# Second mixer of a two-layer block: where each LayerNorm's transposes stand beside the batch's two products

## The chip, the cores and the metric

The kernel runs on 1 core of one Trainium2 chip. The metric is the device time of one execution in microseconds; the kernel before took 2007.04 us, the median of 3 runs (2003.31 to 2009.59). TensorE is called PE below, VectorE DVE, ScalarE ACT, GpSimd POOL and SyncE SP.

## The reference, cut to what matters

Two layers, each `x = x + ga * mixer(LN(x)(1+ca)+sa)` and then `x = x + gb * ffn(LN(x)(1+cb)+sb)`, on x of 4 batches x 512 tokens x 512 features. Layer 0 has linear attention and a mixture of 8 experts. Layer 1, where the change lies, has

```
mixer(h) = h + rmsnorm(y) * norm_w
y        = h @ M          # M (512 x 512): both projections and the elementwise coefficients, made in the kernel
ffn(h)   = sparsify_2to4(silu(h @ w_gate) * (h @ w_up)) @ w_down      # inner size 2048, 2 largest of each 4 kept
```

So one batch of the second mixer is `x += ga*h + rmsnorm(h @ M)*norm_w*ga`: a dense product for y, a product of h with a diagonal matrix (the gate) for `ga*h`, and the root mean square of y.

## The kernel before, in words

Five queues run one hand-written order (`walk`): prologue, 8 groups x 4 batches of attention (stage A), routing, 39 expert slots, `back`, then `step_c` for 4 batches (stage C, the second mixer), then `step_d` for 4 groups x 4 batches (stage D, the second feed-forward), and an end. Every engine has its own list in that order, and they meet on counted semaphores only.

Each float32 product is made of three matmuls on a high and a low part (`mm3`, L744 to L746). A product of 512 tokens therefore needs its input normalised, transposed and split. For one LayerNorm, named (k, b) by kind and batch (k = 2 is the mixer's, k = 3 the feed-forward's), the steps are: DVE takes mean and variance (`c_stats`) and runs a chain of 11 or 12 tiny operations for the scales (`c_scales`); ACT writes the four normalised tiles into `xw` or `xn` (`ln_scaled`, L1373); PE makes 16 transposes of 128x128 into four PSUM slots (`ln_transposes`, L775); ACT takes each slot to `tmp` (L1171) and rounds it to the high part of `hT` (L1175) (`ln_out`); POOL subtracts for the low part (`lo_part`, L2053). `need_h` makes PE wait for the last of these.

The PSUM slots are a ring of two banks (`TAIL`). Everything that passes through the ring has a number from `plan_ring`, the same for all engines; slot n may be written once slot n-2 has been read. The LayerNorm's slots are read by ACT, the diagonal product's four slots ("res") by DVE, which adds them to x (L1970).

In `back`, PE makes M (64 matmuls of 512 columns from `mst`, L1030) and then the transposes of LayerNorms (2,0) and (2,1).

In `step_c(b)`, PE does y (4 tiles of 12 matmuls of 128x512 into six PSUM banks), then the diagonal product `gated_h` (4 tiles of 12 matmuls of 128x128, into ring slots), then the 16 transposes of the LayerNorm in `C_LNS[b]`. ACT first normalises the next LayerNorm, then squares and sums the four y tiles (`squares`, L1383), then empties the transposes. DVE does the statistics, then the scale chain for both the LayerNorm and y (it waits for the squares, L1928), then the four adds that empty the ring (L1970), then scales y into `yn` (L1975), and adds it to x (L1982). POOL marks the res slots and makes the low parts.

In the first `step_d(0, 0)`, r = 0 to 3 counts the four gate/up pairs of a group (24 matmuls of 128x512 each, weights in W1a and W1b). The transposes of (3,1), (3,2) and (3,3) stand behind r = 0, 1 and 3 (`D_LNS`). After r = 3 DVE runs the 2:4 selection on the four products (L2006 to L2033). PE's pair r may begin when DVE has emptied pair r-2 (`d_h`), also across batches.

Of the kernel before, what the change touches and what calls it, by code (L numbers as in the profile page):

```python
# [55 lines left out]
MOD_FINISH = [(0, 1, 2), (3,), (4,), (9,)]  # L56
MOD_PLACE = [(0, 0), (0, 1), (0, 2), (1, 0), (1, 2), (2, 0), (2, 1), (2, 2), (3, 0), (3, 2)]

C_LNS = [(2, 2), (2, 3), (3, 0), None]
D_LNS = {0: (3, 1), 1: (3, 2), 3: (3, 3)}  # L60
STATS = [(2, 0), (2, 1), (2, 2), (2, 3), ("y", 0), (3, 0), ("y", 1), (3, 1), ("y", 2), (3, 2), ("y", 3), (3, 3)]

NSA, NSE, NSD = 4, 4, 6
# [68 lines left out]
def tail_of(stage, g, b):  # L132
# [5 lines left out]
    if isinstance(g, int) and g == 0:  # L138
# [5 lines left out]
ROUTES = [("rt", 0), ("pf", 0)]  # L144
FRONT = [("rt", 1), ("tail", *LAST_A), ("ln", 1, 2, 0), ("ln", 1, 2, 1), ("pf", 1), ("rt", 2),
         ("ln", 1, 3, 0), ("ln", 1, 3, 1), ("pf", 2), ("rt", 3), ("pf", 3)]
BACK = [("ln", 2, b, h) for b in range(2) for h in range(2)]


def plan_ring():  # L150

    at, n = {("ln", 0, 0, 0): 0, ("ln", 0, 0, 1): 2}, 4
    size = {"tail": NT, "ln": NC // 2, "mod": 1, "rt": 1, "pf": 1, "res": NT}
    for stage, groups in (("A", GA), ("B", 0), ("C", 1), ("D", GD)):
        for part in FRONT + BACK if stage == "B" else []:
            at[part] = n
            n += size[part[0]]
        for g in range(groups):
            for b in range(NB):
                tail, ln = tail_of(stage, g, b), layernorms(stage, g, b)  # L160
                parts = [("tail", *tail)] if tail else []
                if ln:

                    halves = [("ln", *ln, 0), ("ln", *ln, 1)]
                    parts = halves[:1] + parts + halves[1:]
                if stage == "C":
                    parts = [("res", b)] + ([("ln", *C_LNS[b], h) for h in range(2)] if C_LNS[b] else [])
                if (stage, g, b) == ("D", 0, 0):
                    parts = [("ln", *ln, h) for ln in D_LNS.values() for h in range(2)]
                if stage == "A" and g == 0:  # L170
                    mods = [[("mod", *use) for use in mod_uses(0, b, k)] for k in range(3)]
                    parts = mods[0] + mods[1] + (halves if ln else []) + mods[2] + ([("tail", *tail)] if tail else [])
                if (stage, g, b) == LAST_A:
                    parts = ROUTES + parts
                for part in parts:
                    at[part] = n
                    n += size[part[0]]
    at[("tail", "D", GD - 1, 3)] = n
    return at
# [51 lines left out]
def build(nc, x_in, wa, wbe, wdn, winout, coef, cT, wmod0, wmod1, gwT, bo, norm_w, out, rows_d_):  # L231
# [4 lines left out]
    with ExitStack() as ctx:  # L236
# [504 lines left out]
        def _(pe):  # L741
# [280 lines left out]
            def back():  # L1022
                pe.wait_ge(m_scaled, 8)
                for half, banks in ((0, (0, 1)), (1, (4, 5))):
                    if half == 0:
                        pe.wait_ge(s_p, SLOTS)
                    for ic in range(8):
                        for j in range(2):
                            m = 2 * half + j
                            last = pe.matmul(bank[banks[j]][:, :], mst[:, ic, m * P:(m + 1) * P], mst[:, ic, 512:1024],  # L1030
                                             start=ic == 0, stop=ic == 7)
                    last.then_inc(m_full, 1)
                for b in range(2):
                    for half in range(2):
                        ln_transposes((2, b), half)

            def gated_h(b):

# [9 lines left out]
            def step_c(b):  # L1048
                need_h(2, b)
                if b == 0:  # L1050
                    pe.wait_ge(m_lo, 4)
                    pe.wait_ge(y_evac, SLOTS)
                for t in range(NT):
                    n = NT * b + t
                    if n >= 6:
                        pe.wait_ge(y_read, n - 5)
                    for c in range(NC):
                        last = mm3(bank[YB[n % 6]][:, :], hcol(c, b, t), lambda h, c=c: M[:, h, c, :],
                                   c == 0, c == NC - 1)
                    last.then_inc(y_full, 1)  # L1060
                gated_h(b)
                for half in range(2):
                    ln_transposes(C_LNS[b], half)


            def tail_d(g, b, n0):
# [11 lines left out]
            def step_d(g, b):  # L1078
                s = g * NB + b
                first = isinstance(g, int) and g == 0  # L1080
                if first:
                    need_h(3, b)
                for r in range(4):
                    if first and b == 0 and r < 2:
                        pe.wait_ge(y_read, (NT * NB - 4, NT * NB)[r])
                    if b == 0:
                        pe.wait_ge(split_done, split_d_at(g, r) + 1)
                    if not (first and b == 0 and r < 2):
                        pe.wait_ge(d_h, s * 4 + (r - 1))
                    for u, o, full in ((0, bank[r % 2], dg_full), (1, bank[4 + r % 2], du_full)):  # L1090
                        for c in range(NC):
                            last = mm3(o[:, :], lambda h, c=c: gud[r // 2][:, r % 2, h, u, c, :], hrow(c, b),
                                       c == 0, c == NC - 1)
                        last.then_inc(full, 1)
                    if first and b == 0 and r in D_LNS:
                        ln_transposes(D_LNS[r], 0)
                        ln_transposes(D_LNS[r], 1)
                tails("D", g, b)

            def epi():  # L1100
# [6 lines left out]
        def _(act):  # L1107
# [236 lines left out]
            def back():  # L1344
# [14 lines left out]
                ln_out((2, 0), 0)  # L1359
                ln_out((2, 0), 1)  # L1360
                ln_scaled(2, 1)
                ln_out((2, 1), 0)
                ln_out((2, 1), 1)

            def ln_scaled(k, b):

# [19 lines left out]
            def step_c(b):  # L1386
                if b > 0:
                    ln_scaled(*((2, 3), (3, 0), (3, 1))[b - 1])
                squares(b)
                if b == 0:  # L1390
                    ln_scaled(2, 2)
                if b == 3:
                    act.wait_ge(ring_full, RING[("res", 3)] + NT)
                    split_d(0, 2)
                    split_d(0, 3)
                if C_LNS[b]:
                    ln_out(C_LNS[b], 0)
                    ln_out(C_LNS[b], 1)

            def step_d(g, b):  # L1400
                s = g * NB + b
# [13 lines left out]
                for r in range(4):  # L1415
# [6 lines left out]
                    if b == 3 and not (isinstance(g, int) and g == GD - 1):  # L1422
                        act.wait_ge(du_full, s * 4 + (r + 1))
                        split_d(g + 1, r)
                    if first and b == 0:
                        if r in D_LNS:
                            if r > 0:
                                ln_scaled(*D_LNS[r])
                            ln_out(D_LNS[r], 0)
                            ln_out(D_LNS[r], 1)  # L1430
                    elif r > 0:
                        absolute(r - 1)
                for r in range(4) if first and b == 0 else (3,):
                    absolute(r)
                if tail_of("D", g, b):
                    act.wait_ge(ring_full, ring_before("D", g, b) + NT)
                if first and b == 0:
# [12 lines left out]
        def _(dve):  # L1450
# [504 lines left out]
            def step_c(b):  # L1955
                if b == 0:
                    c_stats(2, 2)
                    c_stats(2, 3)
                    c_scales((2, 2), (2, 3), ("y", 0))
                else:  # L1960
                    c_stats(3, b - 1)
                    c_scales((3, b - 1), ("y", b))
                n0 = RING[("res", b)]
                for t in range(NT):
                    n = n0 + t
                    if t == 0:
                        dve.wait_ge(ring_read, n)
                    dve.wait_ge(ring_full, n + 1)
                    xt = x[:, NT * b + t, :]
                    dve.tensor_tensor(xt, TAIL[n % 2][:, :], xt, ALU.add).then_inc(ring_read, 1)  # L1970
                dve.wait_ge(crow_full, 16 * (b + 1))
                col = column(("y", b))
                for t in range(NT):
# [10 lines left out]
            def step_d(g, b):  # L1984
                s = g * NB + b
                for r in range(4):
                    dve.wait_ge(du_full, s * 4 + (r + 1))
                    dve.wait_ge(d_silu, s * 4 + (r + 1))
                    dve.tensor_tensor(hh[:, r, :], hh[:, r, :], bank[4 + r % 2][:, :], ALU.mult).then_inc(d_h, 1)  # L1989
                    if isinstance(g, int) and g == 0 and b == 0 and r == 1:  # L1990
                        c_stats(3, 3)
                        c_scales((3, 3))
                done = [0]
# [57 lines left out]
        def _(pool):  # L2051
# [244 lines left out]
            def back():  # L2296
                split_d(0, 0)
                split_d(0, 1)
                for b in range(2):
                    ln_out((2, b), 0)  # L2300
                    ln_out((2, b), 1)

            def step_c(b):
                n0 = RING[("res", b)]
                for t in range(NT):
                    pool.wait_ge(ring_done, n0 + t)
# [2 lines left out]
                if b == 3:  # L2309
                    split_d(0, 2)  # L2310
                    split_d(0, 3)
                ln_out(C_LNS[b], 0)
                ln_out(C_LNS[b], 1)

            def step_d(g, b):
                s = g * NB + b
# [1 line left out]
                    for j in range(4):  # L2318
                        split_d(g + 1, j)
                if isinstance(g, int) and g == 0 and b == 0:  # L2320
                    for ln in D_LNS.values():
                        ln_out(ln, 0)
                        ln_out(ln, 1)
                tails("D", g, b)
                for r in range(4):
                    if isinstance(g, int) and g == GD - 1 and b == NB - 1:
# [63 lines left out]
```

## Time and profile before

| | before |
|---|---|
| median of 3 runs | 2007.04 us |
| the profiled execution: its own time / its span | 2002.69 us / 2000.9 us |
| mean granted PE clock | 0.953 of 2.4 GHz |
| busy: PE / DVE / ACT / POOL | 92% / 60% / 36% / 34% |

"Busy" is the share of the span in which an engine executed something; a row of the timeline has the start in us from the span's start, the duration, engine, source line, operation and tiles, the count where like ones are merged, and in square brackets the idle time before it with the instruction that ended it. The granted clock is 1.00 at 2.4 GHz and 0.50 at 1.2 GHz; a value between is a stretch that had both. Stage C with its run-up lies between 1310 and 1412 us, the first step of stage D between 1412 and 1467.

### The profile page before, as it was taken

The page shows a single profiled execution, that of the slowest core. Times are in us where ns is not written, and L with a number is a line of the kernel's source. Part 1 is how long each engine was busy: PE and PEld are TensorE (multiplying, and loading weights), DVE is VectorE, ACT ScalarE, POOL GpSimd, SP SyncE. Part 2 cuts the span into 40 slices and gives each one's busy share as a digit, 9 for nine tenths or more (in the row PEclk, how much of TensorE's full clock was granted, in tenths as well). Part 3 has the DMA queues.
Part 4 walks back from the last instruction along what each step waited for, and adds up shares of the span by engine and source line. Part 5 has one row for each costly group of instructions (what it writes and reads, how often), then busy time and mean ns, then how long its engine had stood idle before and what let it go on. Part 6 is the DMA issues. An engine that isn't in the chain of part 4 may idle for free. (4 is left out here: it accounts for less than half of the span.)

```text
span 2000.9 us, 25863 instructions
## 1 busy us (share of the span) xinstructions
PE 1842.2 (92%) x8492; PEld 1450.2 (72%) x8492; DVE 1191.6 (60%) x2112; ACT 716.7 (36%) x1369; POOL 686.3 (34%) x697
## 2 busy tenths in 40 slices
PE   8989999999999999998457898989889999999996
PEld 5657888888888888876356676657768778787784
DVE  4557666666666666677853343647465747566664
ACT  2434454445444444433112232355523122213220
POOL 1435121212112222111353555533344445435442
PEclk9999999999999999998758998988999999999998
DMA  6221454435353525421375999610001011101011
GB/s 237 79 71 60 138 159 130 152 95 164 90 189 105 189 82 186 126 85 37 106 258 162 334 267 261 159 52 11 27 27 42 17 32 48 31 5 53 6 53 42
DMA packets 101122, 218.46 MB, mean 109 GB/s; under 512 B 8640, under 2 KB 33232, under 8 KB 99504
## 3 DMA queue, kind: packets, MB, share of 16 engines
q1 hardware_dynamic: 78848, 168.70, 26.0%
q0 software_dynamic: 11584, 28.97, 6.1%
q10 hardware_dynamic: 10608, 19.74, 3.1%
q8 instruction: 45, 0.74, 0.1%
q14 instruction: 37, 0.30, 0.0%
HBM read 126.02 MB, written 91.37 MB: 109 GB/s over the span
## 5 line engine op out<-in xcount | busy, mean ns | idle before, releaser
L744 PE MATMUL bank<-hT,W1b 128*128 128x512 f32 x512 | 208.9, 408 | 14.8 <-DVE hh L1989 14.8
L1743 DVE RECIPROCAL rr<-rr 128x256 f32<-128x256 f32 x128 | 218.8, 1730 | 4.7 <-ACT num L1212 4.7
L744 PE MATMUL bank<-W1a,hT 128*128 128x512 f32 x512 | 209.7, 410 | 3.4 <-DVE hT L1657 3.4
L745 PE MATMUL bank<-hT,W1b 128*128 128x512 f32 x512 | 204.0, 399 | 0.0
L746 PE MATMUL bank<-hT,W1b 128*128 128x512 f32 x512 | 203.6, 398 | 0.0
L746 PE MATMUL bank<-W1a,hT 128*128 128x512 f32 x512 | 202.0, 395 | 0.0
L745 PE MATMUL bank<-W1a,hT 128*128 128x512 f32 x512 | 201.2, 393 | 0.0
L2115 POOL TENSOR_TENSOR x<-x,tmp 128x512 f32<-128x512 f32 x64 | 101.3, 1583 | 272.2 <-DVE tmp L1735 272.2
L1989 DVE TENSOR_TENSOR hh<-hh,bank 128x512 f32<-128x512 f32 x64 | 43.4, 686 | 195.4 <-PE bank L746 166.0
L1762 DVE SCALAR_TENSOR_TENSOR kt<-bank,kt 128x256 fp32r<-128x256 f32 x128 | 50.8, 397 | 173.9 <-ACT vt L1228 173.7
L2053 POOL TENSOR_TENSOR W<-stage,W 128x1024 fp32r<-128x1024 f32 x32 | 76.9, 2404 | 189.5 <-ACT W L1131 187.2
L1227 ACT ACTIVATE kt<-bank 128x256 fp32r<-128x256 f32 x128 | 49.3, 385 | 235.7 <-PE bank L746 235.0
L1441 ACT ACTIVATE ad<-hh 128x512 fp32r<-128x512 f32 x64 | 40.3, 633 | 255.3 <-DVE hh L2033 255.3
L744 PE MATMUL bank<-W1b,ot 128*128 128x512 f32 x256 | 104.8, 410 | 23.0 <-DVE tmp L1732 14.8
L744 PEld LDWEIGHTS bank<-hT,W1b 128*128 128x128 f32 x512 | 97.6, 191 | 38.9 <-DVE hh L1989 17.5
L744 PEld LDWEIGHTS bank<-W1a,hT 128*128 128x128 f32 x512 | 97.2, 190 | 37.0 <-issue 15.5
L746 PEld LDWEIGHTS bank<-hT,W1b 128*128 128x128 f32 x512 | 97.3, 190 | 23.9
L746 PEld LDWEIGHTS bank<-W1a,hT 128*128 128x128 f32 x512 | 97.1, 190 | 22.1
L745 PEld LDWEIGHTS bank<-hT,W1b 128*128 128x128 f32 x512 | 97.5, 190 | 19.8
L744 PE MATMUL bank<-W,ad 128*128 128x512 f32 x256 | 102.8, 402 | 9.0 <-DVE ad L2040 8.9
L745 PEld LDWEIGHTS bank<-W1a,hT 128*128 128x128 f32 x512 | 97.4, 190 | 17.7
L1796 DVE SCALAR_TENSOR_TENSOR qt<-bank,qt 128x512 fp32r<-128x512 f32 x64 | 44.0, 690 | 102.6 <-ACT qt L1256 102.6
(274 smaller groups left out, 4644.0 us busy)
## 6 DMA issues: line engine op xcount, KB each, us to landing
hs_d<-bor SPq DMA_DIRECT2D x24, 1548.0 KB, 11.3
ws_d<-W SPq DMA_DIRECT2D x48, 512.0 KB, 6.3
WB<-ws_d SPq DMA_DIRECT2D x8, 3072.0 KB, 17.9
stage<-wa SPq DMA_DIRECT2D x32, 512.0 KB, 5.3
stage<-wbe SPq DMA_DIRECT2D x24, 512.0 KB, 4.2
stage<-wdn SPq DMA_DIRECT2D x24, 512.0 KB, 3.9
mw<-wmod SPq DMA_DIRECT2D x10, 1024.0 KB, 5.0
hg<-hs_d ACTq DMA_DIRECT2D x39, 258.0 KB, 5.7
```

Of the source, the lines that this page charges most:

```text
L744: pe.matmul(o, lhs(HI), rhs(HI), start=start, stop=False, **kw)
L745: pe.matmul(o, lhs(HI), rhs(LO), start=False, stop=False, **kw)
L746: return pe.matmul(o, lhs(LO), rhs(HI), start=False, stop=stop, **kw)
L1227: act.activation(kt[:, t % 2, HI, :], bank[t % 2][:, 0:256], ACT.Relu)
L1441: act.activation(ad[:, r, HI, :], hh[:, r, :], ACT.Copy).then_inc(d_hi, 1)
L1743: dve.reciprocal(rr[:, pair, h], rr[:, pair, h]).then_inc(r_rec, 1)
L1762: dve.scalar_tensor_tensor(out=kt[:, t % 2, LO, :], in0=bank[t % 2][:, 0:256], scalar=0.0, in1=kt[:, t % 2, HI, :].bitcast(F32), op0=ALU.m ...
L1796: dve.scalar_tensor_tensor(out=qt[:, LO, pair, :], in0=bank[pair][:, :], scalar=0.0, in1=qt[:, HI, pair, :].bitcast(F32), op0=ALU.max, op1 ...
L1989: dve.tensor_tensor(hh[:, r, :], hh[:, r, :], bank[4 + r % 2][:, :], ALU.mult).then_inc(d_h, 1)
L2053: return pool.tensor_tensor(dst, src, hi.bitcast(F32), ALU.subtract)
L2115: pool.tensor_tensor(xt, xt, tmp[:, (key + t) % 2, :], ALU.add).then_inc(ring_done, 1)
```

## The change

Each LayerNorm of the mixer moves one place earlier in the order, each batch's transposes stand between y and the diagonal product, DVE's adds stand ahead of its scale chain, and the three LayerNorms of `step_d(0, 0)` stand behind r = 0 (two) and r = 1 (one). No instruction is added or taken out.

```diff
-C_LNS = [(2, 2), (2, 3), (3, 0), None]
-D_LNS = {0: (3, 1), 1: (3, 2), 3: (3, 3)}
+C_LNS = [(2, 1), (2, 2), (2, 3), (3, 0)]
+D_LNS = [[(3, 1), (3, 2)], [(3, 3)], [], []]
-BACK = [("ln", 2, b, h) for b in range(2) for h in range(2)]
+BACK = [("ln", 2, 0, h) for h in range(2)]
 # plan_ring
-                    parts = [("res", b)] + ([("ln", *C_LNS[b], h) for h in range(2)] if C_LNS[b] else [])
+                    parts = [("ln", *C_LNS[b], h) for h in range(2)] + [("res", b)]
...
 # PE, back
-                for b in range(2):
-                    for half in range(2):
-                        ln_transposes((2, b), half)
+                for half in range(2):
+                    ln_transposes((2, 0), half)
 # PE, step_c
-                gated_h(b)
                 for half in range(2):
                     ln_transposes(C_LNS[b], half)
+                gated_h(b)
 # PE, step_d
-                    if first and b == 0 and r in D_LNS:
-                        ln_transposes(D_LNS[r], 0)
-                        ln_transposes(D_LNS[r], 1)
+                    if first and b == 0:
+                        for ln in D_LNS[r]:
+                            ln_transposes(ln, 0)
+                            ln_transposes(ln, 1)
 # ACT, back
                 ln_scaled(2, 1)
-                ln_out((2, 1), 0)
-                ln_out((2, 1), 1)
 # ACT, step_c
                 squares(b)
+                ln_out(C_LNS[b], 0)
+                ln_out(C_LNS[b], 1)
                 if b == 0:
                     ln_scaled(2, 2)
                 if b == 3:
                     act.wait_ge(ring_full, RING[("res", 3)] + NT)
                     split_d(0, 2)
                     split_d(0, 3)
-                if C_LNS[b]:
-                    ln_out(C_LNS[b], 0)
-                    ln_out(C_LNS[b], 1)
 # ACT, step_d, after silu of pair r
-                    if first and b == 0:
-                        if r in D_LNS:
-                            if r > 0:
-                                ln_scaled(*D_LNS[r])
-                            ln_out(D_LNS[r], 0)
-                            ln_out(D_LNS[r], 1)
-                    elif r > 0:
+                    for ln in D_LNS[r] if first and b == 0 else []:
+                        if ln != (3, 1):
+                            ln_scaled(*ln)
+                        ln_out(ln, 0)
+                        ln_out(ln, 1)
+                    if first and b == 0 and r == 2:
+                        absolute(0)
+                    if r > (1 if first and b == 0 else 0):
                         absolute(r - 1)
-                for r in range(4) if first and b == 0 else (3,):
-                    absolute(r)
+                absolute(3)
 # DVE, step_c: the chain goes behind the four adds
-                    c_scales((2, 2), (2, 3), ("y", 0))
...
-                    c_scales((3, b - 1), ("y", b))
...
                     dve.tensor_tensor(xt, TAIL[n % 2][:, :], xt, ALU.add).then_inc(ring_read, 1)
+                c_scales(*([(2, 2), (2, 3)] if b == 0 else [(3, b - 1)]), ("y", b))
 # DVE, step_d
-                    if isinstance(g, int) and g == 0 and b == 0 and r == 1:
+                    if isinstance(g, int) and g == 0 and b == 0 and r == 0:
                         c_stats(3, 3)
                         c_scales((3, 3))
```

POOL's `back`, `step_c` and `step_d` follow the same order: `ln_out(C_LNS[b])` moves to the head of `step_c`, ahead of the res marks and of `split_d(0, 2)` and `split_d(0, 3)`.

## Rows read from the trace of the kernel before

**Rows 1.** The page, part 1: engine, busy us (share of the span), instructions.

```profile
PE 1842.2 (92%) x8492; PEld 1450.2 (72%) x8492; DVE 1191.6 (60%) x2112; ACT 716.7 (36%) x1369; POOL 686.3 (34%) x697
```

**Rows 2.** Busy time by stretch: stretch, length, busy us (instructions) by engine, clock, DMA.

```profile
1335.40:1347.70 12.30, 10.70 (x66) 9.55 (x64) 7.69 (x21) 6.33 (x10) 2.01 (x5) 0.72 0.00 0
1358.70:1370.50 11.80, 10.34 (x67) 9.16 (x65) 7.79 (x21) 3.46 (x7) 2.13 (x6) 0.75 0.00 1
1382.00:1392.70 10.70, 9.25 (x65) 8.10 (x64) 7.38 (x21) 3.20 (x6) 1.78 (x5) 0.84 0.00 0
1403.70:1412.00 8.30, 7.05 (x51) 6.87 (x49) 3.91 (x15) 0.69 (x2) 0.55 (x3) 0.82 0.00 0
1417.00:1443.70 26.70, 23.36 (x115) 18.43 (x114) 13.94 (x26) 17.58 (x27) 11.89 (x9) 1.00 0.12 38
```

**Rows 3.** Timeline of PE, run-up and stage C.

```profile
1314.16 0.66 PE L775 MATMUL bank<-ident,xw 128*128 128x128 f32 x4 [0.67 <-ACT tmp L1171]
1320.56 3.15 PE L775 MATMUL bank<-ident,xnb 128*128 128x128 f32 x12 [5.74 <-ACT xnb L1373]
1324.33 0.48 PE L744 MATMUL bank<-M_,hT 128*128 128x512 f32 x1
...
1335.41 0.22 PE L744 MATMUL bank<-dg,hT 128*128 128x128 f32 x1
1337.93 0.27 PE L746 MATMUL bank<-dg,hT 128*128 128x128 f32 x1
1339.58 0.33 PE L744 MATMUL bank<-dg,hT 128*128 128x128 f32 x1 [1.38 <-DVE x L1970]
...
1340.75 0.41 PE L745 MATMUL bank<-dg,hT 128*128 128x128 f32 x1
1343.52 0.41 PE L746 MATMUL bank<-dg,hT 128*128 128x128 f32 x1
...
1358.78 0.22 PE L744 MATMUL bank<-dg,hT 128*128 128x128 f32 x1
...
1382.01 0.22 PE L744 MATMUL bank<-dg,hT 128*128 128x128 f32 x1
...
1403.79 0.22 PE L744 MATMUL bank<-dg,hT 128*128 128x128 f32 x1
```

**Rows 4.** Timeline of DVE, batch 0: head of the chain, then the adds.

```profile
1336.40 0.17 DVE L1928 TENSOR_SCALAR cst<-csum 128x4 f32<-128x4 f32 x1 [17.35 <-ACT sqj L1383]
...
1338.84 1.29 DVE L1970 TENSOR_TENSOR x<-bank,x 128x512 f32<-128x512 f32 x2
```

**Rows 5.** Timeline of ACT: slots 1 and 3 of (2,0), and the last square of batch 0.

```profile
1311.99 0.78 ACT L1171 ACTIVATE tmp<-bank,modc 128x512 f32<-128x512 f32 x1
...
1314.91 0.78 ACT L1171 ACTIVATE tmp<-bank,modc 128x512 f32<-128x512 f32 x1
...
1335.61 0.60 ACT L1383 ACTIVATE sqj<-bank 128x512 bf16<-128x512 f32 x1 [2.06 <-PE bank L746]
```

**Rows 6.** Timeline of POOL: the last two low parts of (2,0).

```profile
1316.43 2.59 POOL L2053 TENSOR_TENSOR hT<-tmp,hT 128x512 fp32r<-128x512 f32 x2 [0.32 <-ACT hT L1175]
```

**Rows 7.** Timeline of PE, first step of stage D.

```profile
1411.97 0.73 PE L744 MATMUL bank<-hT,W1a 128*128 128x512 f32 x1
...
1415.88 0.39 PE L744 MATMUL bank<-hT,W1a 128*128 128x512 f32 x1
...
1419.33 1.03 PE L775 MATMUL bank<-ident,xnb 128*128 128x128 f32 x8
...
1422.59 0.48 PE L744 MATMUL bank<-hT,W1a 128*128 128x512 f32 x1
```

**Rows 8.** Timeline of ACT, one LayerNorm normalised, stage D.

```profile
1426.36 2.92 ACT L1373 ACTIVATE xw<-x,cst 128x512 f32<-128x512 f32 x4
```

**Rows 9.** Timeline of DVE: the first selection begins.

```profile
1452.29 0.85 DVE L2006 TENSOR_TENSOR fl<-xnb 128x512 bf16<-128x512 f32 x1 [7.47 <-ACT xnb L1413]
```

**Rows 10.** Timeline of PE: the third pair of batch 1 begins.

```profile
1466.76 0.79 PE L744 MATMUL bank<-hT,W1b 128*128 128x512 f32 x1 [7.49 <-DVE hh L1989]
```

More of the change, by code:

```diff
@@ L166, in plan_ring @@
                 if stage == "C":
-                    parts = [("res", b)] + ([("ln", *C_LNS[b], h) for h in range(2)] if C_LNS[b] else [])
+                    parts = [("ln", *C_LNS[b], h) for h in range(2)] + [("res", b)]
                 if (stage, g, b) == ("D", 0, 0):
-                    parts = [("ln", *ln, h) for ln in D_LNS.values() for h in range(2)]
+                    parts = [("ln", *ln, h) for lns in D_LNS for ln in lns for h in range(2)]
                 if stage == "A" and g == 0:
@@ L2298, in back @@
                 split_d(0, 1)
-                for b in range(2):
-                    ln_out((2, b), 0)
-                    ln_out((2, b), 1)
+                ln_out((2, 0), 0)
+                ln_out((2, 0), 1)
             def step_c(b):
+                ln_out(C_LNS[b], 0)
+                ln_out(C_LNS[b], 1)
                 n0 = RING[("res", b)]
@@ L2311, in step_c @@
                     split_d(0, 3)
-                ln_out(C_LNS[b], 0)
-                ln_out(C_LNS[b], 1)
             def step_d(g, b):
@@ L2320, in step_d @@
                 if isinstance(g, int) and g == 0 and b == 0:
-                    for ln in D_LNS.values():
-                        ln_out(ln, 0)
-                        ln_out(ln, 1)
+                    for lns in D_LNS:
+                        for ln in lns:
+                            ln_out(ln, 0)
+                            ln_out(ln, 1)
                 tails("D", g, b)
```

## The prediction

> **What bounds the kernel now.** I read the page first: PE is busy for 92% of the span, the next engine for 60% [rows 1], so what counts is where PE waits and at which clock it runs. Next the stretches around the change: in each batch of stage C the part behind y runs at a granted clock of 0.72 to 0.84, while the first step of stage D, three sets of transposes included, runs at 1.00 [rows 2]. Then the timeline of PE, to see why. I call E(b) the moment when y of batch b is issued and what follows it begins: E(0) to E(3) are 1335.41, 1358.78, 1382.01 and 1403.79 [rows 3]. In batch 0 the first two diagonal tiles go out as 24 matmuls, the last of them 2.52 us behind the first: 0.11 us each. The third waits 1.38 us for DVE, which is in its scale chain from 1336.40 to 1338.8 and only then empties the ring [rows 3, 4]. The other three batches have the same wait. The reader is to see what comes behind it: from 1340.75 the same matmuls take (1343.52 - 1340.75) / 13 = 0.213 us. The clock has gone from 2.4 to 1.2 GHz, 5.3 us after E(0), behind two tiles that keep PE half fed and one short wait. Rows 2 say the same of the other batches.
>
> **The change part by part.**
>
> *Start of the stage.* Before, PE stood still from 1314.6 until ACT had normalised (2,1), made its transposes at 1320.56 and began y(0) at 1324.33 [rows 3]. Now y(0) needs only (2,0), whose last low part POOL ends at 1316.43 + 2.59 = 1319.02 [rows 6]. y takes 1335.41 - 1324.33 = 11.08 us [rows 3]. PE has then idled for 4.5 us and starts slow. The nearest price is the first pair of stage D: nine matmuls from 1411.97 to 1415.88 took 3.91 us [rows 7] where nine at the full clock take 9 x 11.08 / 48 = 2.08, a loss of 1.8. E(0) comes at 1319.1 + 11.1 + 1.8 = 1332.0: 3.4 us earlier (5.2 without the slow start).
>
> *Behind y: the transposes.* The last square begins 0.20 us behind E and lasts 0.60 [rows 5] and 0.15 to 0.35 for reading out its sum and changing over, so ACT takes the first slot at E + 0.95. It takes the third slot 2.92 us after the first and needs 0.78 for it [rows 5]: E + 4.65. The diagonal product's first slot is the one that follows that, so it cannot start before E + 4.7, where before it started at E. Up to there PE has only 16 transposes, some 1.65 us of work. That is 3.0 us of idle in three pieces of 0.9 to 1.2.
>
> *The diagonal product.* DVE has nothing in front of the adds now and empties a tile in 0.65 [rows 4] against 1.34 for making one: the 1.38 us wait goes, in four batches. At the full clock the 48 matmuls take 5.35 us and end at E + 10.1; need_h is met (POOL ends at about E + 8 to 9, its four low parts 7.0 us behind ACT's first slot as in rows 5 and 6). At 1.2 GHz they take 48 x 0.213 = 10.2 and end at E + 14.9.
>
> *Which clock.* This decides. In all four batches of before the clock fell during the diagonal product, with 1.38 us or less of idle beside it [rows 2, 3]. The new order puts 3.0 us of idle right ahead of the same half-fed matmuls, so I expect a fall no later than before. The rows against it are those of stage D, where 16 transposes took 3.26 us [rows 7], 1.6 of it idle, and the clock stayed at 1.00 [rows 2]; but there dense pairs stand on both sides. I take the fall at E + 5.3, the soonest of the four: 0.6 us at full clock (5 matmuls), then 43 x 0.213 = 9.1. The product ends at E + 14.4. The bounds are 10.1 and 14.9. Then y of the next batch begins slow, again 1.8 (0 to 2.8).
>
> The Trainium skill (TensorE: Matmul & The Clock Gate, "HAM oscillation") lays the fall to one long idle gap. By that rule the gaps of 1.2 us here would do nothing, and the first rival below would be the outcome; this case's trace disagrees, since its clock fell behind 1.38 us. The same page ("A second HAM failure mode") says that many micro-idles between groups of matmuls make the clock swing, and with that the trace agrees.
>
> *Sum to E(3).* A batch takes 14.4 + 11.1 + 1.8 = 27.3 us; three are 81.9, where before E(0) to E(3) was 68.38 [rows 3]: +13.5. DVE keeps up: its chain (2.4), yn (2.7), adds to x and statistics end 12 us behind the product, in y's shade, where nothing waits.
>
> *Into stage D.* From E(3) to the end of pair 0 it was 1419.33 - 1403.79 = 15.54 us [rows 3, 7], without a LayerNorm between. Now it has one: 14.4 + 5.5 + 1.8 = 21.7, +6.2. At the end of pair 0 we stand at -3.4 + 13.5 + 6.2 = +16.3.
>
> *First step of stage D*, from the end of pair 0, T. Before: 1466.76 - 1419.33 = 47.4 until PE resumes behind the selection [rows 7, 10]. Now two LayerNorms stand behind pair 0, but ACT normalises (3,2) only when it has emptied (3,1): 0.7 + 5.8 + 2.9 [rows 5, 8] = T + 9.45, while PE is through with (3,1) at T + 3.3 [rows 7]. PE idles 6.2 us and the transposes run slow (3.8, as 1320.56 to 1324.33 [rows 3]): T + 13.4. Pair 1 takes 5.6 + 0.9 (half a slow start), a wait of 0.8 for (3,3), its transposes 3.3, pairs 2 and 3 11.2: T + 35.2 against T + 28.8 before. Here the work was not on the path: before, the selection began only at 1452.29, T + 33.0, as ACT had (3,3) to do first [rows 9]. Now it begins 1.0 behind pair 3, at T + 36.2, and from there to the resumption it is 1466.76 - 1452.29 = 14.5 [rows 9, 10]: T + 50.7, +3.3 (2 to 5). The remaining steps of stage D only shift.
>
> *DMA.* None is added. SP's loads of crow and of the next weights keep their places in its queue and wait for the same events; with a DMA share of 0.00 beside the mixer [rows 2] I count them at nothing. POOL makes two weight splits (5 us) behind the res marks of batch 3 as before, and pair 2 is the first to need them.
>
> *Total.* 16.3 + 3.3 = +19.6 us. Against the profiled execution's own 2002.69 that is 2022.3. That execution lies 4.35 under the median of the three runs, 2007.04, and the sum upon the median is 2026.6. I say 2024. It splits as -5.0 + 6.1 for each batch whose clock falls, since one at the full clock takes 10.1 + 11.1 = 21.2 instead of 27.3.
>
> **The rivals.**
>
> 1. *The clock holds (other side).* PE's transposes and the unbroken diagonal product keep 2.4 GHz. Then 3 x 21.2 = 63.6 against 68.4, with -3.4 at the start, nothing between E(3) and T (10.1 + 5.5), +3.3 in stage D: -5.0, 1998 to 2002. It decides if fewer than one batch in four falls. For it: the wait of 1.38 is gone and stage D's transposes never cost the clock. Against: 3.0 us of idle take its place.
> 2. *The clock falls in half of the batches*, or late in each: -5.0 + 2 x 6.1 = +7.2, 2012.
> 3. *The clock holds, and stage D costs all of its PE delay*, the selection giving no cover: 35.2 - 28.8 = 6.4 in place of 3.3: -1.9, about 2003, no change.
>
> **How the numbers follow.** Forecast 0.60, rival 1 0.17, rival 2 0.15, rival 3 0.08. All four batches slow for the whole product with a slow start of 2.8 gives 2 x 4 = 8 us more, 2034; the forecast's own range is 2012 to 2034. Reaching to the rivals the range is 2003 to 2034. Within 0.3% (6 us, about what a measurement tells) lie rival 3 and half of rival 1: 0.15. Rival 1's faster half and what I have missed: 0.11. Slower: 0.74.
>
> **What would show it.** Granted clock between E and the next y: below 0.75 in each batch if I am right, 1.00 if rival 1 is. First diagonal matmul 4.7 us behind E, with no wait for DVE in it. E(0) near 1332, E to E 27 us (21 for rival 1). PE idle for 6 us ahead of the transposes of (3,2). The selection starting 1 us behind pair 3. I am wrong if the diagonal matmuls are 0.111 us apart throughout, or if the transposes are emptied faster than ACT's pace here.

## The result, and the profile after

The changed kernel takes 2027.25 us (median of 4 runs, 2022.06 to 2029.61), the kernel before 2005.17 on the same chip; the ratio is 1.0104, with a 95% interval of 1.0077 to 1.013. By the ratio that is 21 us slower (22 between the two medians). The forecast was 2024. The profiled execution took 2027.44 us, with a span of 2025.7, and the mean granted clock went from 0.953 to 0.944.

The stretches that answer to [rows 2], each from E to 16.7 us behind it, and then the first step of stage D in two parts (columns as there):

```profile
1334.70:1351.40 16.70, 14.44 (x71) 13.23 (x70) 4.05 (x12) 5.99 (x10) 5.82 (x8) 0.66 0.00 1
1362.20:1378.90 16.70, 14.44 (x71) 13.25 (x70) 3.93 (x12) 5.99 (x10) 5.81 (x8) 0.66 0.00 0
1389.70:1406.40 16.70, 14.44 (x70) 13.34 (x69) 3.79 (x11) 5.99 (x10) 5.82 (x8) 0.65 0.00 0
1417.20:1433.90 16.70, 14.44 (x70) 13.35 (x69) 3.72 (x8) 7.74 (x12) 6.44 (x9) 0.64 0.01 6
...
1439.20:1453.00 13.80, 6.04 (x34) 4.50 (x32) 13.63 (x22) 11.02 (x16) 7.26 (x5) 0.75 0.13 38
...
1461.30:1466.00 4.70, 3.94 (x19) 3.11 (x19) 0.00 (x0) 3.70 (x6) 2.35 (x2) 0.68 0.00 0
```

The clock falls in all four batches. The timeline of PE shows how in batch 0; it answers to [rows 3]:

```profile
1321.22 0.80 PE L744 MATMUL bank<-M_,hT 128*128 128x512 f32 x1 [4.25 <-POOL hT L2049]
...
1334.74 1.03 PE L775 MATMUL bank<-ident,xnb 128*128 128x128 f32 x8
1336.35 0.66 PE L775 MATMUL bank<-ident,xnb 128*128 128x128 f32 x4 [0.57 <-ACT tmp L1171]
1337.68 0.66 PE L775 MATMUL bank<-ident,xnb 128*128 128x128 f32 x4 [0.67 <-ACT tmp L1171]
1339.35 0.30 PE L744 MATMUL bank<-dg,hT 128*128 128x128 f32 x1 [1.01 <-ACT tmp L1171]
...
1340.18 0.41 PE L745 MATMUL bank<-dg,hT 128*128 128x128 f32 x1
...
1348.71 0.41 PE L746 MATMUL bank<-dg,hT 128*128 128x128 f32 x1
1348.92 0.73 PE L744 MATMUL bank<-M_,hT 128*128 128x512 f32 x1
1349.46 0.63 PE L745 MATMUL bank<-M_,hT 128*128 128x512 f32 x1
1349.88 0.63 PE L746 MATMUL bank<-M_,hT 128*128 128x512 f32 x1
```

E(0) is 1334.74. The diagonal product starts 4.6 us later, and no DVE wait is left in it. From E + 5.4 its matmuls are 0.213 us apart, and it ends at E + 14.2; in the other batches the clock falls at E + 5.4, 5.1 and 4.9, and the product ends at E + 14.3 to 14.7. The next y begins at 0.43 us a matmul instead of 0.23. E to E is 27.48, 27.50 and 27.50 us.

"Half-fed" is short for this: a 128x128 matmul goes out every 0.111 us at the upper clock and every 0.213 us at the lower one, a 128x512 matmul every 0.23 and 0.43 us. So the diagonal product needs about half of the time for a quarter of the columns.

In stage D (answers to [rows 7, 10], timeline of PE) there are the idle of 6.3 us ahead of (3,2), and one of 2.6 ahead of (3,3):

```profile
1439.23 1.03 PE L775 MATMUL bank<-ident,xnb 128*128 128x128 f32 x8
...
1449.06 3.15 PE L775 MATMUL bank<-ident,xw 128*128 128x128 f32 x12 [6.33 <-ACT xw L1371]
...
1461.33 1.09 PE L775 MATMUL bank<-ident,xnb 128*128 128x128 f32 x8 [2.64 <-ACT xnb L1371]
...
1492.06 0.80 PE L744 MATMUL bank<-hT,W1b 128*128 128x512 f32 x1 [4.07 <-DVE hh L1985]
```

Times within the stage are best counted from the first transposes of (2,0), S, because S itself lies anywhere from 1309.9 to 1315.7 in the profiled executions of these kernels. I call T the end of pair 0 and R the resumption behind the first selection. Before, S is 1310.82, the start of those transposes in that trace.

| | S to E(0) | E(0) to E(3) | E(3) to T | T to R | S to R |
|---|---|---|---|---|---|
| before | 24.6 | 68.4 | 15.5 | 47.4 | 155.9 |
| after | 21.8 | 82.5 | 22.0 | 52.8 | 179.1 |

S to R costs 23.2 us more in these two executions.

### The profile page after: what moved, and what is told of

The parts are those of the page before. It is cut to its first block and busy times, and to the rows that moved or that the text cites. A ratio compares the mean times of both kernels' runs of the same rounds, so it can differ in the third digit from the quotient of the medians.

```text
span 2025.7 us, 25863 instructions
## 1 busy us (share of the span) xinstructions
PE 1857.0 (92%) x8492; PEld 1465.2 (72%) x8492; DVE 1186.8 (59%) x2112; ACT 716.0 (35%) x1369; POOL 682.4 (34%) x697
## 5 line engine op out<-in xcount | busy, mean ns | idle before, releaser
L744 PE MATMUL bank<-W1b,ot 128*128 128x512 f32 x256 | 105.2, 411 | 21.9 <-DVE tmp L1729 14.1
L744 PEld LDWEIGHTS bank<-hT,W1b 128*128 128x128 f32 x512 | 97.8, 191 | 35.4 <-DVE hh L1985 14.1
L745 PEld LDWEIGHTS bank<-hT,W1b 128*128 128x128 f32 x512 | 97.6, 191 | 19.8
```

Of the source, the lines that this page charges most:

```text
L744: pe.matmul(o, lhs(HI), rhs(HI), start=start, stop=False, **kw)
L745: pe.matmul(o, lhs(HI), rhs(LO), start=False, stop=False, **kw)
```

## The experiments

Theory 1 is that of the prediction: the clock, pulled down by idle ahead of the half-fed diagonal product. Theory 2 is that this product is slow for its place, and the clock a consequence. All ratios are to the kernel before, run on the same chip.

**All gaps filled** (`fill_all`). The changed kernel, with matmuls whose result nobody reads. `fill(4)` also stands between slots 3 and 4 and behind the last; `fill` first waits until `yn` has read the bank, which the cut leaves out:

```diff
+def fill(count):        # into a y bank that yn has read (the wait is left out here)
+    for _ in range(count):
+        pe.matmul(bank[YB[(NT * b + 4) % 6]][:, :], hT[:, HI, 0, b * S:b * S + P], M[:, HI, 0, :], start=True, stop=True)
 ln_transposes(C_LNS[b], 0)
+fill(4)
```

> The changed kernel with 4 idle-filling matmuls of 128x512 (0.23 us each, results never read) in each of the three gaps of the transposes behind y: 12 per batch, 48 in all, more work for PE and nothing removed. Theory 1 (the loss is the clock, which falls because 3 us of idle stand ahead of the half-fed diagonal product): granted clock 1.00 between E and the next y, diagonal matmuls 0.111 us apart, E to E 21.1 instead of 27.5 us, and about 24 us less than the changed kernel: about 2003, ratio to the kernel before 0.998 to 1.001. Theory 2 (the diagonal product is slow for its place in the order or for the slots it waits for, and the clock only follows): E to E stays at 27.5 us or grows by the fillers, ratio 1.010 or more.

Measured: 1998.40 us, ratio 0.9966 (0.9952 to 0.9979). Busy time by stretch, E(0) and 10 us:

```profile
1333.60:1343.60 10.00, 10.00 (x78) 9.14 (x76) 2.08 (x3) 6.00 (x10) 5.68 (x7) 1.00 0.01 2
```

Twelve more matmuls a batch, and a batch takes 21.1, 21.3 and 21.1 us instead of 27.5, with the diagonal product where the change put it, waiting for the same slots. Theory 2 is out. The gain over the changed kernel is 1.4%, some 28 us, 4 more than expected; 2.4 of these lie between T and R. Dummy matmuls do two things at once: they take idle away and add dense work. This run doesn't tell which of the two held the clock.

**Only the last gap filled** (`fill_last`).

```diff
 ln_transposes(C_LNS[b], 1)
+fill(4)
 gated_h(b)
```

At the other two places `fill(0)` stands: no matmul, but its wait for `yn` is there. The first gap is 0.66 to 0.93 us in batches 1 to 3, against 0.57 in the changed kernel.

> The changed kernel with 4 such matmuls in the last of the three gaps alone, directly ahead of the diagonal product; 2 us of idle stay. Theory 1, if what counts is the idle just ahead of the diagonal product: the clock holds in all four batches, as with all gaps filled (ratio about 1.000). Theory 1, if the whole stretch counts: it holds in some batches and falls in others (ratio 1.003 to 1.008). Theory 2: ratio 1.010 or more.

Measured: 1999.32 us, ratio 0.9980 (0.9965 to 0.9995); the clock is 1.00 in all four stretches, of which batch 1's is

```profile
1354.60:1365.00 10.40, 8.74 (x70) 7.76 (x69) 2.52 (x8) 6.44 (x12) 5.69 (x7) 1.00 0.00 0
```

A third of the dummy work, directly ahead of the diagonal product, is enough: 1.3 to 1.7 us of idle stay in each stretch and do nothing.

**The kernel before, its one wait filled** (`before_fill`). Five such matmuls between the second and the third diagonal tile, again behind a wait for a free bank.

```diff
 for t in range(NT):          # gated_h
+    if t == 2:
+        fill(5)
```

> The kernel before with 5 idle-filling matmuls of 128x512 (0.23 us each, results never read) where PE waits 1.3 us for DVE between the second and the third diagonal tile. If that one idle is what makes the clock fall in the kernel before, it now holds: E to E 21 us instead of 23.4, 23.2 and 21.8, and with E(3) to the end of pair 0 at 12.5 instead of 15.5 about 8 us less, ratio 0.996. If the half-fed diagonal product alone does it: ratio 1.000 and the same granted clock of 0.72 to 0.84 behind E.

Measured: 1996.04 us, ratio 0.9962 (0.9950 to 0.9974), and 21.5, 21.4 and 21.4 us a batch. So in the kernel before the clock did not fall for the diagonal product alone, but only with that wait in it. `adds_first` below shows the same without any added work. Answers to the first row of [rows 2]:

```profile
1335.80:1346.20 10.40, 9.06 (x70) 7.77 (x69) 7.25 (x21) 6.11 (x10) 1.76 (x5) 1.00 0.00 0
```

**The stage D part undone** (`d_undone`). ACT's absolute values and DVE's chain for (3,3), one pair later, stand as before too.

```diff
-D_LNS = [[(3, 1), (3, 2)], [(3, 3)], [], []]
+D_LNS = [[(3, 1)], [(3, 2)], [], [(3, 3)]]
```

> The changed kernel with the part in the first step of stage D undone: (3,1), (3,2), (3,3) behind pairs 0, 1, 3 as before. If the stage D part costs what the changed kernel's trace shows (52.8 us from the end of pair 0 to the resumption, where before it was 47.4), 5.4 us come back: about 2021, ratio 1.0075. If the idle there was hidden by the selection, as rival 3 has it in reverse, nothing moves: ratio 1.010.

Measured: 2020.23 us, ratio 1.0092 (1.0064 to 1.0121); T to R is 46.7 us, 6.1 less than in the changed kernel, and S to R falls by the same 6.1. The interval overlaps that of the changed kernel, so the ratios alone would allow no gain; the stretch shows it, in one profiled execution of each. With all gaps filled as well (`fill_d_undone`):

> The changed kernel with all three gaps filled (as in the first of these runs) and the stage D part undone. If the two terms are independent, the ratio is that of the filled kernel, 0.9966, less the 3 to 5 us of the stage D part: 0.994 to 0.995. If the selection covers the stage D part once the clock holds: 0.9966.

Measured: 1998.20 us, ratio 0.9971 (0.9956 to 0.9986), the same as `fill_all`. T to R is 50.4 in `fill_all`, 49.5 in `fill_last` and 49.4 here, so at most 1.0 us is left of the stage D part: with the clock held, T comes before DVE has yn of batch 3, and pair 1 waits 1.38 us for it and then runs slow for its first nine matmuls (7.3 us for the pair). The two terms are not independent.

**The DVE part undone** (`chain_first`). The scale chain ahead of the adds again, in the changed kernel.

```diff
+c_scales(*([(2, 2), (2, 3)] if b == 0 else [(3, b - 1)]), ("y", b))
 for t in range(NT):          # the four adds
...
-c_scales(*([(2, 2), (2, 3)] if b == 0 else [(3, b - 1)]), ("y", b))
```

> The changed kernel with the DVE part undone: the scale chain stands ahead of the four adds again. Theory 1 (in the new PE order the adds cannot begin before E + 7, and the chain needs only E + 0.9 to E + 3.3, so the part that the change is named for does nothing there): E to E stays at 27.5 us and the ratio to the kernel before at 1.010; yn is ready 2.4 us earlier, which may give back up to 2 us in the first step of stage D. Theory 2 (the adds ahead of the chain carry a gain of their own, 4 x 1.3 us, hidden by the clock's loss): 5 us slower than the changed kernel, 1.0125.

Measured: 2020.88 us, ratio 1.0071 (1.0047 to 1.0095). A batch takes 27.5, 27.7 and 27.5 us, as before this edit; T to R falls from 52.8 to 48.5. The two ratios' intervals overlap, but the stretch shows it: in the new PE order the DVE part of the change brings nothing and costs 4 us. The timelines of DVE and POOL say how, first in the changed kernel:

```profile
1433.28 4.91 POOL L2049 TENSOR_TENSOR W1b<-stage,W1b 128x1024 fp32r<-128x1024 f32 x2
...
1433.36 2.32 DVE L1929 TENSOR_TENSOR cst<-cst 128x8 f32<-128x8 f32 x1
1435.92 2.30 DVE L1931 SCALAR_TENSOR_TENSOR cst<-cst 128x8 f32<-128x8 f32 x1
...
1439.54 2.72 DVE L1971 SCALAR_TENSOR_TENSOR yn<-bank,cst,crow 128x512 f32<-128x512 f32 x4
1442.17 6.11 DVE L1978 TENSOR_TENSOR x<-x,yn 128x512 f32<-128x512 f32 x4
...
1448.80 2.46 DVE L1908 BATCH_NORM_STATS2 st<-x 128x6 f32<-128x512 f32 x4
...
1458.15 0.16 DVE L1933 SCALAR_TENSOR_TENSOR cst<-cmv,cst 128x4 f32<-128x4 f32 x1
```

and with the DVE part undone:

```profile
1434.28 2.72 DVE L1971 SCALAR_TENSOR_TENSOR yn<-bank,cst,crow 128x512 f32<-128x512 f32 x4
...
1442.28 2.46 DVE L1908 BATCH_NORM_STATS2 st<-x 128x6 f32<-128x512 f32 x4
...
1449.42 0.16 DVE L1933 SCALAR_TENSOR_TENSOR cst<-cmv,cst 128x4 f32<-128x4 f32 x1
```

In the changed kernel batch 3's chain stands behind the adds and runs while POOL splits weights (1433.28 to 1438.2), and two of its 0.17 us operations take 2.3. yn begins at T + 0.3 instead of T - 6.2, the scales of (3,3) are there at T + 18.9 instead of T + 9.0, PE waits 2.64 us instead of 0.78, and loses the clock once more (0.68 above; 1.00 in `chain_first`). The Trainium skill (SBUF — State Buffer, "SBUF: two separate sides") says that VectorE and GpSimd share a port pair, and that whichever of a VectorE instruction with two inputs in SBUF and a GpSimd instruction that reads SBUF starts first keeps it for its whole length. The rows agree: the stretched operations take both inputs from `cst` and end with POOL's two subtractions of 2.45 us, while yn in `chain_first`, which reads a PSUM bank, takes 0.68 us a tile beside the same weight split (1434.80 to 1440.0 there), as it does in the changed kernel without it.

`chain_first` shows one thing more. In its batches 2 and 3 the clock is down at the first diagonal matmul:

```profile
1395.69 0.44 PE L744 MATMUL bank<-dg,hT 128*128 128x128 f32 x1 [1.01 <-ACT tmp L1171]
1395.94 0.42 PE L745 MATMUL bank<-dg,hT 128*128 128x128 f32 x1
```

So behind y the 16 transposes with their three gaps are enough for the fall, without any half-fed matmul.

**DVE's order alone, on the kernel before** (`adds_first`).

```diff
 if b == 0:
     c_stats(2, 2)
     c_stats(2, 3)
+    c_scales((2, 2), (2, 3))
-else:
-    c_stats(3, b - 1)
-c_scales(...)
 # the four adds
+if b > 0:
+    c_stats(3, b - 1)
+c_scales(*([(3, b - 1)] if b > 0 else []), ("y", b))
```

> The kernel before with one part of the change alone: DVE empties the diagonal product's slots ahead of the scale chain (and of the next statistics; in batch 0 the LayerNorm's part of the chain runs early by itself). The order on PE stays as it was: y, diagonal product, transposes. Theory 1: without the wait of 1.3 us no idle stands beside the diagonal product, so the clock holds too: E to E falls from 23.4, 23.2 and 21.8 to 19.8 us and E(3) to the end of pair 0 from 15.5 to 11.0: 13 us less than before, about 1992, ratio 0.9935. If the diagonal product alone pulls the clock down, only the waits go: 5 us less, ratio 0.9975. If DVE becomes late for its new order (adds, statistics, chain, yn and x need 17 to 20 us of a batch): between the two or no gain.

Measured: 1997.72 us, ratio 0.9982 (0.9968 to 0.9996). The clock holds through the four batches, with nothing added to PE's work: the wait was what pulled it down in the kernel before. But yn is late: two batches wait 0.9 us, and pair 1 of stage D 4.24. It was the third case. So in the next one (`stats_first`) the statistics stay ahead of the adds, and only the chain stands behind them:

```diff
     c_scales((2, 2), (2, 3))       # batch 0
+else:
+    c_stats(3, b - 1)
 # the four adds
-if b > 0:
-    c_stats(3, b - 1)
 c_scales(*([(3, b - 1)] if b > 0 else []), ("y", b))
```

> The kernel before with DVE's order of the change (statistics, adds, then one scale chain) and batch 0's LayerNorm scales taken early; PE's order as before: y, diagonal product, transposes. The run with the adds ahead of the statistics kept the clock at 1.00 but made PE wait for yn: 0.9 us in two batches and 4.2 us in front of pair 1. With the statistics taken ahead of the adds these go: 6 us less than that run, about 1991 to 1992, ratio 0.994 to 0.995, E to E 19.9 us. If the waits for yn stay: 0.998.

Measured: 1991.01 us, ratio 0.9933 (0.9914 to 0.9953), 19.9 us a batch, E(3) to T 10.8. The waits for yn in the batches are gone, one of 1.37 us ahead of pair 1 is left.

**Transposes inside y** (`inside_y`), and all of them behind tile 1 (`mid_y`). In the changed kernel, with stage D as before and batch 0's scales early:

```diff
 # PE, inside the loop over the tiles t of y; ACT's ln_out likewise behind its square t
+if t in {0: (0,), 2: (1,)}:        # mid_y: {1: (0, 1)}
+    ln_transposes(C_LNS[b], 0 if t == 0 else 1)
...
-for half in range(2):
-    ln_transposes(C_LNS[b], half)
 gated_h(b)
```

> The change rearranged: each LayerNorm's 16 transposes stand inside y, 8 behind tile 0 and 8 behind tile 2, the diagonal product directly behind y; ACT empties them between its squares; DVE as in the change with batch 0's LayerNorm scales taken early; stage D as before. No matmul waits for a ring slot, and what idle is left stands between dense tiles. Theory 1: granted clock 1.00 through the four batches, 5.4 + 11.1 + 1.6 = 18.1 us a batch, the end of pair 0 at 20 us earlier than in the kernel before, some 1 to 2 us given back to a wait for yn: about 1986, ratio 0.990 to 0.992. If DVE is the next bound (adds, chain, yn, x, statistics: 17 to 20 us a batch): 19.5 to 20 us a batch, ratio 0.994.

> The same, but with all 16 transposes together behind tile 1 of y. The same two gaps of about 0.9 us for ACT's emptying are there as in the changed kernel, between dense tiles instead of ahead of the diagonal product. Theory 1 (it is the place of the idle, ahead of half-fed matmuls, that costs the clock): granted clock 1.00, 19.9 us a batch, ratio 0.993 to 0.995. If these gaps cost the clock wherever they stand: a granted clock under 0.9 in the batches, 22 us or more a batch, ratio above 0.998.

Measured: `inside_y` 1988.28 us, ratio 0.9916 (0.9892 to 0.9939), the lowest of all, though its interval overlaps that of `stats_first`; 18.1 us a batch with PE busy for the whole of it. `mid_y` 1999.15 us, ratio 0.9968 (0.9951 to 0.9986); 19.8, 21.1 and 22.7 us. First `inside_y`, then two batches of `mid_y` (the rows behind a long gap, then the stretches):

```profile
1357.20:1375.30 18.10, 18.10 (x113) 16.02 (x112) 12.73 (x33) 9.91 (x19) 5.06 (x8) 1.00 0.07 16
```

```profile
1368.62 0.66 PE L775 MATMUL bank<-ident,xnb 128*128 128x128 f32 x4 [1.83 <-ACT tmp L1172]
1389.67 0.66 PE L775 MATMUL bank<-ident,xw 128*128 128x128 f32 x4 [1.82 <-ACT tmp L1172]
```

```profile
1354.80:1375.90 21.10, 18.59 (x114) 16.09 (x113) 12.74 (x33) 10.80 (x20) 5.91 (x8) 1.00 0.04 14
1375.90:1398.50 22.60, 20.10 (x113) 17.14 (x113) 12.74 (x33) 10.88 (x20) 5.86 (x8) 0.92 0.03 12
```

In `mid_y` the gaps of batch 1 (0.57 and 0.68 us) leave the clock alone. In batches 2 and 3 ACT is late, the gaps are 1.83 and 0.68, and the clock falls in the second of the two and not in the first. So theory 1 in its strict form, that the place alone counts, is too strong: the amount seems to count too, and equal batches can differ. Executions differ as well: the seven lie between 1992.48 and 2002.59 us, and the profiled one took 1993.24. The wait ahead of pair 1 is another such pair: 1.38 us behind the same gaps, and the clock falls in `fill_d_undone` but holds in `stats_first`, `inside_y` and `mid_y` (1.37 to 1.38 us; 5.7 to 5.8 us for the pair, against 7.3). What decides between them no run shows.

From S to R, against 155.9 before, these profiles have: `fill_all` 151.1, `fill_last` 150.2, `before_fill` 147.8, `d_undone` 173.0, `fill_d_undone` 150.6, `chain_first` 174.6, `adds_first` 150.5, `stats_first` 142.8, `inside_y` 136.3, `mid_y` 147.3. The timed ratios, turned into us on 2005, lie within 5 us of these differences.

## Why the prediction was right

*Start of the stage.* Forecast 3.4 us earlier, measured 24.6 - 21.8 = 2.8: y(0) began after 4.25 us of idle (4.5), and the slow start cost 2.4 us instead of 1.8 (y took 13.52).

*Transposes and slots.* Right: the diagonal product at E + 4.6 (forecast 4.7). Its 3.0 us of idle are counted from issue to issue; as the profile counts, by which the wait before was 1.38, the three gaps are 2.25 us.

*The clock.* Right, and this carried the result: the fall at E + 4.9 to 5.4 (forecast 5.3, taken from the soonest row of before), in four of four batches, 0.213 us a matmul, the end at E + 14.2 to 14.7 (14.4), a slow start of y of 1.9 to 2.2 (1.8), a batch of 27.5 us (27.3). Three runs show it from both sides: filling the idle takes the loss away in the changed kernel and takes the old loss away in the kernel before; `adds_first` and `stats_first` take the wait itself away and the clock holds. For the changed kernel no run takes the gaps away and leaves the order, so that idle and not missing dense work is the cause there is argued from these. The prediction gave the half-fed product a share in the fall; `chain_first` shows that it isn't needed. And [rows 2] show two sets of stage D's transposes at 1.00, not three as the prediction has it; the third lies behind their window.

By the rule of one long idle gap of the Trainium skill (TensorE: Matmul & The Clock Gate, "HAM oscillation") the clock should have held, since no gap behind y exceeded 1.01 us; the measurement decides against it. By the same page of the Trainium skill ("A second HAM failure mode") frequent short idles between groups of matmuls make the clock swing; with three gaps a batch it did. In the kernel before a single wait a batch was enough, so the agreement that the prediction saw there was loose.

*Into stage D.* 22.0 us against the forecast 21.7.

*First step of stage D.* The idle ahead of (3,2) was 6.3 (6.2), and the selection began right behind pair 3, but at T + 38.5 and not T + 36.2, and T to R was 52.8 and not 50.7. The step that failed is "DVE keeps up": its chain, yn, adds to x and statistics were said to end where nothing waits. That holds for batches 0 to 2, not for batch 3, whose chain fell on POOL's weight split; (3,3) came late. The same sentence hid that the DVE part of the change costs 4.3 us: I counted it as freeing a wait of 1.38 us, but in the new order the first add comes at E + 6.8 to 7.4, and with the chain ahead of it (`chain_first`) the chain was done by E + 5.3 to 6.5. That the term came out only 2.1 too small is luck: with DVE in time T to R is 48.5, so the rest of the term was forecast 2.2 too large (the selection began 0.9 us sooner than forecast, and from there to R it was 13.2 us and not 14.5).

*The sum.* +19.6 forecast; 23.2 between the two profiled executions (-2.8 + 14.1 + 6.5 + 5.4), 21 by the ratio on 2005. All four terms came out above the forecast's -3.4 + 13.5 + 6.2 + 3.3. That 2024 lies as near as it does owes something to the step from 2022.3 towards the higher median. Rival 1 (the clock holds, -5.0) is what `fill_all` made real: -6.8 by its ratio. Rival 2 did not occur. Rival 3's price for stage D, 6.4, turned out near the 6.1 that `d_undone` gave back, but on top of the clock's loss.

The change was aimed at a real loss, the wait of 1.24 to 1.38 us in each batch and the clock that it costs. The PE part put three gaps in its place and turned the gain into a loss. DVE's order alone, with the statistics left ahead and batch 0's LayerNorm scales taken early (`stats_first`), takes 0.67% off.

## What to carry to other kernels

In this kernel one wait of 1.24 to 1.38 us amid half-fed matmuls cost PE its full speed, for up to 1.9 us a batch over the same product with the wait filled, and 2.25 us in three pieces ahead of them cost 6.4. Put short work that waits for another engine's emptying between dense matmuls, and nothing that makes PE wait ahead of narrow ones. When an order is changed, ask of each engine what it now waits for first: here the adds that were moved ahead had nothing to be ahead of.

## What the runs showed of the hardware that was not expected

Dummy matmuls paid for themselves: 4 per batch (`fill_last`), 0.9 us of PE's time that was idle anyway, gained 6.4 us a batch. Taking the wait away in the kernel before (`stats_first`, 142.8 us from S to R) was still better than filling it (`before_fill`, 147.8).

Two alike batches of `mid_y`, with the same gaps of 1.83 and 0.68 us between dense tiles, ran one at 1.00 and one at 0.92.

Tiny DVE operations are not always tiny: 0.17 us became 2.3 beside POOL's 128x1024 subtractions.
